# Stage 2 of a two-stage kernel: transpose of the second normalized row tile by a DMA in place of TensorE

## The reference, cut to what matters

```python
def reference(x, ctx, g_xattn, g_ffn, s1, z1, s2, z2, W_up, gate_w, expert_bias, lora_A, lora_B):
    # x: (2, 1024, 2048) f32, ctx: (2, 2048, 2048), W_up: (2048, 2048), 4 experts of rank 8
    h = x + tanh(g_xattn[0]) * matmul(fake_quant(layernorm(x), s1, z1), fake_quant(ctx, s2, z2))
    y = layernorm(h)
    top1 = argmax(y @ gate_w.T + expert_bias)
    base = y @ W_up.T
    delta = ((y @ lora_A[top1].T) @ lora_B[top1].T)
    return h + tanh(g_ffn[0]) * (base + delta)
```

## Time and profile before

| what | value |
|---|---|
| median of 3 runs | 960.24 us (959.9 to 960.27) |
| the profiled execution | 959.95 us |
| its span (first to last instruction) | 958.1 us |
| PE, DVE, ACT, POOL busy | 936.5, 472.3, 234.5, 17.1 us |
| stage 1, stage 2 | 0 to 260.6 us, 260.6 to 958.1 us |
| products of one tile in stage 2 | 43.2 us |

### The profile page before, as it was taken

How to read it: one execution, slowest core, us unless ns; L and a number is a source line. 1 busy time by engine, 2 the same in 40 slices (tenths; PEclk the granted TensorE clock), 3 DMA queues, 4 the chain that set the end, 5 groups by cost and what they waited for, 6 DMA issues and landing times.

```text
span 958.1 us, 12470 instructions
## 1 busy us (share of the span) xinstructions
PE 936.5 (98%) x5253; PEld 501.1 (52%) x5278; DVE 472.3 (49%) x1022; ACT 234.5 (24%) x196; POOL 17.1 (2%) x40
## 2 busy tenths in 40 slices
PE   3999999999999999999999999999999999999998
PEld 2444444444455555555555555555555555555554
DVE  7774757785884715343342615343342615343321
ACT  6975776777650100000000000000000000000000
POOL 0001100000000000000000000000000000000000
PEclk9999999999999999999999999999999999999999
DMA  8999987688652332222223233222223222121211
GB/s 350 422 405 406 377 318 271 227 302 290 221 152 88 111 110 44 88 44 89 44 89 88 66 111 45 88 44 88 45 88 88 61 72 44 45 45 44 44 44 44
DMA packets 77081, 135.26 MB, mean 141 GB/s; under 512 B 61936, under 2 KB 62080, under 8 KB 62720
## 3 DMA queue, kind: packets, MB, share of 16 engines
q1 hardware_dynamic: 71088, 92.74, 30.1%
q0 software_dynamic: 3488, 24.92, 6.7%
q10 hardware_dynamic: 2448, 16.78, 4.3%
HBM read 90.38 MB, written 29.37 MB: 125 GB/s over the span
## 4 chain that ended last, share of the span: by engine, by line
PE 96%; ACT 2%; DVE 1%; DMA 1%; issue 0%; SPq 0%; ACTq 0%
PE bank L1085 71%; PE bank L1003 22%; PE bank L1094 1%; PE bank L980 1%; ACT arena L414 1%; DMA rows<-in_x 1%; DVE bn L598 0%; ACT rows_T L402 0%; ACT halves L384 0%; PE bank L1077 0%; DVE arena L669 0%; SPq L282 0%; PE bank L1100 0%; DVE ln L602 0%; ACT ln L378 0%
## 5 line engine op out<-in xcount | busy, mean ns | idle before, releaser
L1085 PE MATMUL bank<-arena,rows_T 128*128 128x416 f16 (+1 forms) x3840 | 683.4, 339 | 0.0
L1085 PEld LDWEIGHTS bank<-arena,rows_T 128*128 128x128 f16 x3840 | 372.4, 97 | 304.3
L1003 PE MATMUL bank<-arena,rows_T 128*128 128x512 bf16 x999 | 222.8, 381 | 3.7 <-DVE arena L669 2.5
L1003 PEld LDWEIGHTS bank<-arena,rows_T 128*128 128x128 bf16 x1024 | 99.5, 98 | 120.6 <-issue 4.8
L783 DVE SCALAR_TENSOR_TENSOR rows<-bank,derived,rows 128x416 f32<-128x416 f32 (+2 forms) x80 | 49.8, 640 | 213.9 <-PE bank L1085 213.9
L453 ACT ACTIVATE z_stack_T<-bank 96x128 f16<-96x128 f16 x16 | 4.4, 273 | 560.1 <-PE bank L1100 560.1
L598 DVE BATCH_NORM_STATS2 bn<-rows 128x6 f32<-128x512 f32 x124 | 76.7, 678 | 5.9 <-DMA rows<-in_x 5.7
L723 DVE SCALAR_TENSOR_TENSOR route<-bank,derived,scal 128x4 f32<-128x4 f32 x16 | 3.5, 221 | 113.2 <-PE bank L1085 113.2
L659 DVE SCALAR_TENSOR_TENSOR rows<-bank,derived,rows 128x512 f32<-128x512 f32 x60 | 44.7, 748 | 25.0 <-PE bank L1003 24.6
L791 DVE SCALAR_TENSOR_TENSOR rows<-bank,z_back_scale,rows 128x512 f32<-128x512 f32 x64 | 45.1, 746 | 10.6 <-PE bank L1094 6.6
L699 DVE SCALAR_TENSOR_TENSOR halves<-normed,ln,halves 128x2048 f16<-128x2048 f32 x14 | 32.9, 2351 | 29.0 <-ACT halves L447 29.0
(11 more groups left out here) (106 smaller groups left out, 293.0 us busy)
## 6 DMA issues: line engine op xcount, KB each, us to landing
arena<-in_ctx SPq DMA_DIRECT2D x22, 1024.0 KB, 16.4
stage<-in_w SPq DMA_DIRECT2D x17, 1042.0 KB, 5.5
out<-rows ACTq DMA_DIRECT2D x15, 1024.0 KB, 3.9
h_scratch<-rows POOLq DMA_DIRECT2D x11, 1024.0 KB, 9.5
rows<-h_scratch SPq DMA_DIRECT2D x11, 1024.0 KB, 4.9
stage<-in_ctx SPq DMA_DIRECT2D x10, 1024.0 KB, 9.9
rows<-in_x POOLq DMA_DIRECT2D x10, 1024.0 KB, 9.2
normed<-in_w SPq DMA_DIRECT2D x7, 1042.0 KB, 6.5
```

Of the source, the lines that this page charges most:

```text
L1003: mm = mmul(bk, q1T[:, t % 4, kt, :], Q(b, n, kt), start=(kt == 0), stop=(kt == KT - 1 and not slow), skip_group_check=True)
L1085: mm = mmul(bank[c][:, 0:b - a], YT[:, s % 2, yh, kt, :], W(kt, wh, a, b), start=(first and kt == kts[0] and yh == 0 and wh == 0), stop=(k ...
```

## The change

The constant BY_PE becomes 1, and a new one, UNSCALED = 2, takes its place where the question is whether y was multiplied by `WR`. Tile 1 keeps its unscaled halves, and its transposes go from TensorE to a DMA. yT_out(1, g) multiplies in place, from `rows_T` to `rows_T`. On SP this transpose comes after L306 and its wait and ahead of L310, and SP waits for it; POOL's last load waits for it too. On DVE yT_out(1, 2) and yT_out(1, 3) move ahead of epi2(0, 3) and epi2(0, 4).

```diff
-    BY_PE = 2
+    BY_PE = 1
+    UNSCALED = 2
@@ PSUM views of the transposes
-        YB = [[TR[0], TR[1], bank[7][:, :], TR[0]], [TR[0], TR[1], TR[0], TR[1]]]
+        YB = [TR[0], TR[1], bank[7][:, :], TR[0]]
@@ sync
+            def y_transpose(s):
+                sp.wait_ge(s_yl, s + 1)
+                if s == 1:
+                    sp.wait_ge(s_mm, place[(TILES - 1, NCH - 1)] + 1)
+                else:
+                    sp.wait_ge(s_m2, 5 * (s - 1))
+                sp.dma_start_transpose(YT[:, s % 2].rearrange("p h k m -> p (h k) m"),
+                                       HL[:, :, :].rearrange("p h d -> p (h d)")).then_inc(s_dt, 16)
...
             sp.wait_ge(s_wr0, 16)
-            sp.wait_ge(s_lo, KT)
+            y_transpose(1)
+            sp.wait_ge(s_dt, 16)
             sp.dma_start(WR, ...).then_inc(s_wr, 16)
-            for s in range(BY_PE, TILES):
+            for s in range(UNSCALED, TILES):
                 if s + 3 < TILES:
                     row(TILES + s + 3)
-                sp.wait_ge(s_yl, s + 1)
-                sp.wait_ge(s_m2, 5 * (s - 1))
-                sp.dma_start_transpose(...).then_inc(s_dt, 16)
+                y_transpose(s)
@@ gpsimd
             pool.wait_ge(s_bst, 1)
+            pool.wait_ge(s_dt, 16)
             row(TILES + KEEP)
@@ scalar, y_high; vector, norm and y_low
-                if s < BY_PE:
+                if s < UNSCALED:
@@ vector
             def yT_out(s, g):
-                dve.wait_ge(s_yt, 4 * s + g + 1)
-                if s < 2:
-                    dve.wait_ge(s_mm, place[(13 if s == 0 else 15, NCH - 1)] + 1)
-                src = YB[s][g].bitcast(F16).rearrange("p (h a m) -> p h a m", h=2, a=4)
                 dst = YT[:, s % 2, :, 4 * g:4 * g + 4, :]
+                if s < BY_PE:
+                    dve.wait_ge(s_yt, 4 * s + g + 1)
+                    dve.wait_ge(s_mm, place[(13, NCH - 1)] + 1)
+                    src = YB[g].bitcast(F16).rearrange("p (h a m) -> p h a m", h=2, a=4)
+                else:
+                    dve.wait_ge(s_dt, 16)
+                    src = dst
                 back = wc[:, 4 * g:4 * g + 4].unsqueeze(1).unsqueeze(3).to_broadcast([P, 2, 4, P])
                 v.tensor_tensor(dst, src, back, ALU.mult).then_inc(s_ye, 1)
...
             yT_out(1, 0)
             yT_out(1, 1)
-            for c in range(5):
+            for c in range(3):
                 epi2(0, c)
             yT_out(1, 2)
             yT_out(1, 3)
+            epi2(0, 3)
+            epi2(0, 4)
@@ tensor
             def tile2(s):
-                if s >= BY_PE:
+                if s >= UNSCALED:
                     pe.wait_ge(s_dt, 16 * (s - BY_PE + 1))
...
                 products(0, c, range(LATE, KT), False).then_inc(s_m2, 1)
-                if c == 1:
-                    y_transposes(1, 0)
-                    y_transposes(1, 1)
                 if c == 3:
                     z_transposes(0)
-            y_transposes(1, 2)
-            y_transposes(1, 3)
```

More of the change, by code:

```diff
@@ L308, in _ @@
             sp.wait_ge(s_wr0, 16)
-            sp.wait_ge(s_lo, KT)
+            y_transpose(1)
+            sp.wait_ge(s_dt, 16)
             sp.dma_start(WR, wrow_d.rearrange("k p -> (k p)").unsqueeze(0).to_broadcast([P, D])).then_inc(s_wr, 16)
-            for s in range(BY_PE, TILES):
+            for s in range(UNSCALED, TILES):
                 if s + 3 < TILES:
                     row(TILES + s + 3)
-                sp.wait_ge(s_yl, s + 1)
-                sp.wait_ge(s_m2, 5 * (s - 1))
-                sp.dma_start_transpose(YT[:, s % 2].rearrange("p h k m -> p (h k) m"),
-                                       HL[:, :, :].rearrange("p h d -> p (h d)")).then_inc(s_dt, 16)
+                y_transpose(s)
         @block.gpsimd
@@ L1073, in y_transposes @@
                 else:
-                    pe.wait_ge(s_ye, {0: 1, 1: 4 + g - 1}[s])
+                    pe.wait_ge(s_ye, 1)
                 for i in range(8):
                     h, k = i // 4, 4 * g + i % 4
-                    mm = nc.tensor.transpose(YB[s][g].bitcast(F16)[:, i * P:(i + 1) * P],
+                    mm = nc.tensor.transpose(YB[g].bitcast(F16)[:, i * P:(i + 1) * P],
                                              HL[:, h, k * P:(k + 1) * P], idh[:, :])
```

## The result

The changed kernel takes 958.38 us (median of 22 runs, 957.48 to 959.83) against 960.07 us for the kernel before (22 runs, 959.19 to 961.48). The ratio is 0.9984 with a 95% interval of 0.9977 to 0.999: 1.7 us, or 0.16%, faster, on the small side of the 0.2% named ahead. The prediction was 958.5. The profiled execution went from 959.95 to 958.16 us and its span from 958.1 to 956.4.

What follows compares the result with a forecast made beforehand. TensorE, busy 98% of the span, was taken to bound the kernel. Removing 32 transposes at 56 ns takes 1.78 us, all else adds 0: 960.24 - 1.78 = 958.46, rounded to 958.5 us, range 957.9 to 959.6.

Steps and rivals of the forecast that it cites:

- The sum: Whole kernel: 1.78 us of tile 1's transposes leave TensorE, 0 added, so 960.24 becomes 958.46 us.
- The rival of 220 ns: Tile 1's transposes on TensorE cost their full duration, 32 being 7.0 us, for 953.2 us; chance 0.02.
- The cover: Start of tile 1: the DMA transpose lands in time; TensorE's deadlines, 303.36 and 307.6, are met with 4.1 and 4.8 us spare.
- The deadline: Start of tile 1: TensorE stalls if the DMA transpose lands (L) from 300.4 us on.
- the ends 0.68 and 2.4: DVE's in-place multiply for tile 1: lower and upper bounds in us around 1.21; cost to TensorE 0 by both.
- The steps forecast for 296.25, 298.67, 300.4 and 302.8: DVE before tile 1: first multiply starts, first two end, three epi2 of tile 0 end, last two multiplies end.
- What is moved: WR broadcast and POOL's row load, issued at about 295.4 us, behind the transpose: cost 0, WR with 16 us of cover.
- Faster or same: Chances against the 0.2% (1.92 us) measurable: faster 0.32, same 0.62, slower 0.06.
- The late rival: Start of tile 1: the DMA transpose takes 16.6 us, TensorE stalls 4.9, net +3.1, about 963.3 us; chance 0.05.
- may not be the ones that matter: Rival on the DMA queue: despite the transfers held off, the transpose takes 8.5 us; still 958.5, within the forecast's case.

Runs made afterwards that it cites:

- the fourfold transposes: Kernel before, with each of tile 1's 32 transposes on TensorE done four times: 965.2 us against 960.04, ratio 1.0052.
- the landing at 300.94: Changed kernel with one more DMA transpose of the same size ahead of the real one, each waited for: 958.74 us, ratio 0.9986.
- The kernel whose transpose landed at 305.64: Changed kernel with the WR broadcast issued ahead of tile 1's transpose and POOL's row load not waiting for it: 962.85 us, ratio 1.002.

## Why the prediction was right

**The sum.** Removed 1.78 us, measured 1.69 between the medians and 1.79 between the profiled executions. That 958.5 and 958.38 lie only 0.1 us apart is in part luck: the forecast started from the 960.24 of three runs, where 22 give 960.07. That the price is the spacing of 56 ns was shown by the fourfold transposes (54 to 56 ns). The rival of 220 ns is out. So is, as the price of one in a full stream, the 275 ns of the Trainium skill, "TensorE: Matmul & The Clock Gate", section "Part 4: PE-mode transpose".

**The cover.** Landing forecast for 295.35, measured 294.4: `w_back_row` took 15.4 us instead of 16.6. The transpose took 6.8 us against 6.7 taken. The deadline was put at L = 300.4; the landing at 300.94 with a stall of 0.60 puts it at 300.34.

**DVE.** The in-place multiply was taken at 1.21 us and measured 1.213; the ends 0.68 and 2.4 were not needed. The steps forecast for 296.25, 298.67, 300.4 and 302.8 came at 296.41, 298.68, 300.32 and 302.59.

**What is moved.** WR and the row load began at 294.4 and 295.1, as forecast for about 295.4, and no one waited for them.

**Faster or same.** I gave 0.62 to "within 0.2%" and 0.32 to "faster by more". The measured 0.16% lies in the first, with an interval that reaches from 0.10 to 0.23%.

**Two steps that were off, though they did not decide.** The late rival was priced by the stall alone: landing at 305.25, a stall of 4.9, 963.3 us. The kernel whose transpose landed at 305.64 had the stall, 5.2 us, and took 965.05: after a stall of that length TensorE runs for a while at half clock, 1.8 us here, 1.5 after 7.4 us of idle time, 1.6 after the 2.9 and 0.2 us at the start of stage 2. None of it showed where the stall was 0.6 (granted clock 1.00). And the worth of holding the two transfers back had no price: I wrote that the transfers kept off the queue "may not be the ones that matter" and allowed 8.5 us for the transpose. Let loose together they stretched it to 17.6 in the profiled execution, and the change without that part is slower than the kernel before (ratio 1.002; single executions from 958.57 to 965.47 us). So the gain depends on holding back at least one of the two transfers until the transpose has landed; it doesn't depend on DVE's new order.

The Trainium skill, "VectorE: DVE Perf Modes", section "The three transpose paths", has 1309 ns for one block by DMA. Here 32 blocks in one DMA landed in 6.8 us, 0.21 us each, so the page's rate, taken one block after the other, doesn't hold for a large transpose.

## What to carry to other kernels

On a saturated TensorE, price what you take away by the distance between starts, and work out for each engine that takes over the work the time at which TensorE will want it. Then test that slack by delaying the new step on purpose: here 6.1 us of slack made the change safe, one more megabyte on the DMA queues fit into it and two, in the median, did not. Here the stalls of 3 to 7 us cost more than their length, since TensorE came back at half clock, so in an in-order queue put the new wait behind everything that frees something for TensorE; the same transposes of tile 0 left the kernel 0.9 us slower than before with one order on DVE and 4.2 us faster with another (tile 1's 1.7 us is in both; the second order also moves a sqrt on ACT).

## What had not been expected of the hardware

- In the one execution that was profiled of each kernel, a DMA transpose with two transfers of 1 MB ahead and beside it took 17.6 us to land, with the one ahead 9.3, with the one beside 13.0, alone 6.8. With both, its issue on SP took 15.5 us, with the one ahead 7.3, and 4.8 to 5.0 otherwise. The runs of the kernel with both scatter over 6.9 us, so 17.6 is not a constant price.
- After 3.1 (two waits with 6 products between them), 5.2 and 7.4 us without work TensorE's products ran at a granted clock of 0.50 for a stretch, at a loss of 1.6, 1.8 and 1.5 us; after 0.6 us the clock was 1.00.
